# Token table of the expert layer by one-hot matrix products instead of indirect DMAs, with the mixer's steps in a new order

## What is computed

```python
# 1. linear attention, 16 heads of 32, in chunks of 128 tokens, with a decayed state
x = layernorm(x + rms_norm(lightning_attn(rotary(x @ Wq), rotary(x @ Wk), x @ Wv)) @ Wo)

# 2. a selective scan over the context (512 inner channels, 16 states), gated by silu(x)
u = silu(conv1d(in_proj_w @ ctx, conv_w) + conv_b)          # 4 taps, causal
dt_low, Bm, Cm = split(x_proj_w @ u, [16, 32])
dt = softplus(dt_proj_w @ dt_low + dt_proj_b)
for t in range(512):
    state = state * exp(dt[t] * A) + (dt[t] * u[t]) * Bm[t]
    y[t] = (state * Cm[t]).sum(states)
x = layernorm(x + ((y + D * u) * silu(x)))

# 3. experts: 64, each token goes to its best 8; an expert takes at most 256 tokens
probs = softmax(x @ router_weight.T)
topw, topi = top_k(probs, 8);  topw /= topw.sum()
pos = place of (token, choice) in its expert's list, in order of tokens
xe[topi, pos] = x                      # where pos < 256
ye = (silu(xe @ gate) * (xe @ up)) @ down
y = sum over the 8 choices of ye[topi, pos] * topw          # 0 where pos >= 256
x = layernorm(x + y)
```

## Time and profile before

| | us |
|---|---|
| median of 3 runs (1345.42 to 1348.79) | 1347.47 |
| the profiled execution, its own time | 1349.46 |
| its span in the profile | 1347.6 |

### The profile page before, as it was taken

The page is one execution under the profiler, slowest core; times in us unless marked ns, Lnnn a source line. Parts: engine busy times, 40 slices in busy tenths (PEclk is TensorE's granted clock), DMA queues, the critical chain, the costliest instruction groups (busy, mean ns, idle before and its releaser), DMA issues. The chain is left out here.

```text
span 1347.6 us, 19321 instructions
## 1 busy us (share of the span) xinstructions
PE 1138.9 (85%) x6389; PEld 757.4 (56%) x6389; DVE 1100.1 (82%) x1536; ACT 853.8 (63%) x1536; POOL 1003.9 (74%) x796
## 2 busy tenths in 40 slices
PE   7489997898979779967887718999999999999950
PEld 2234443354424434433443418999999999999940
DVE  2379988989968799878798566998888989898846
ACT  5474585734756444847345326888878888888843
POOL 0778768777899997999988744777777777777644
PEclk9698887997889789878978658999999999999985
DMA  6525425323242432163133306999999999999978
GB/s 244 140 72 191 110 65 145 99 70 83 49 111 61 124 84 51 46 154 106 38 83 102 98 13 208 302 315 305 308 304 306 305 313 301 313 301 311 285 138 326
DMA packets 97490, 235.26 MB, mean 175 GB/s; under 512 B 20704, under 2 KB 21216, under 8 KB 96752
## 3 DMA queue, kind: packets, MB, share of 16 engines
q1 hardware_dynamic: 65648, 162.66, 39.5%
q0 software_dynamic: 31744, 71.37, 22.3%
HBM read 147.48 MB, written 52.94 MB: 149 GB/s over the span
## 5 line engine op out<-in xcount | busy, mean ns | idle before, releaser
L1226 DVE TENSOR_TENSOR_SCAN hst<-hst,dbu 128x512 f32<-128x512 f32 x256 | 299.2, 1214 | 97.1 <-POOL dbu L1035 71.8
L1035 POOL TENSOR_TENSOR dbu<-rep,bc 128x1024 f32<-128x1024 f32 x128 | 301.8, 2360 | 64.1 <-PE y_ps L396 35.3
L1642 POOL DMA_INDIRECT sum_rows<-ye,tokens x128 | 205.5, 1606 | 98.4 <-ACT ye L1721 75.6
L396 PE MATMUL y_ps<-dbu,cs 128*32 128x512 f32 x512 | 167.8, 741 | 70.3 <-DVE dbu L1232 62.6
L799 ACT ACTIVATE hst<-rep,small_sb 128x512 f32<-128x512 f32 x256 | 165.9, 685 | 56.8 <-DVE dbu L1232 51.5
L1634 POOL DMA_INDIRECT xe<-x_rows,tokens x128 | 150.6, 1176 | 61.4 <-issue 37.8
L434 PE MATMUL ring<-first_raw,xT 128*128 128x512 f32 x384 | 176.7, 604 | 0.5 <-DVE x2T L1314 0.5
L1232 DVE TENSOR_TENSOR dbu<-hst,bc 128x1024 f32<-128x1024 f32 x128 | 156.7, 1224 | 4.4
L1684 PE MATMUL low<-xh,w1h 128*128 128x256 f32 x512 | 150.5, 294 | 0.0
L1684 PE MATMUL low<-xh,w1l 128*128 128x256 f32 x512 | 145.3, 284 | 0.0
L1684 PE MATMUL low<-xl,w1h 128*128 128x256 f32 x512 | 145.2, 284 | 0.0
(11 more groups left out here) (198 smaller groups left out, 2680.0 us busy)
## 6 DMA issues: line engine op xcount, KB each, us to landing
first_raw<-in_gate_up SPq DMA_DIRECT2D x64, 768.0 KB, 9.8
rep<-made SPq DMA_DIRECT2D x256, 128.0 KB
second_raw<-in_down SPq DMA_DIRECT2D x64, 256.0 KB, 5.1
bc<-bc_rows SPq DMA_DIRECT2D x64, 128.0 KB, 3.2
second_raw<-in_down SPq DMA_DIRECT2D x64, 128.0 KB, 7.2
rows<-sum_rows SPq DMA_DIRECT2D x16, 512.0 KB, 8.9
sum_rows<-x2T SPq DMA_DIRECT2D x1, 4608.0 KB, 17.2
xT<-in_x_turned SPq DMA_DIRECT2D x16, 256.0 KB, 3.0
```

The lines of the kernel that those rows point to most:

```text
L396: ins = pe.matmul(y_ps[rows, :], sel, dbu[:, n % WORK, g, :], start=(k == 0), stop=(k == QUADS - 1))
L1035: pool.tensor_tensor(dbu[:, n % WORK, :, :], rep[:, i % 2, :, 1, :], bc[:, k, 0, :].unsqueeze(1).broadcast_to([P, 2, T]), ALU.mult).then_i ...
L1226: dve.tensor_tensor_scan(h, h, dbu[:, n % WORK, i, :], 0.0, ALU.mult, ALU.add).then_inc(scanned, 1)
L1642: pool.indirect_dma_start(sum_dram[e % SUMS], bass.IndirectOffsetOnAxis(ap=tokens[:, e, j:j + 1], axis=0), ye[:, e % YE, j, :], None, comp ...
```

## The change

- **All sequences' tables on chip.** The DRAM tables, the indirect DMAs, `tell_slots` and `split_slots` go. `number_slots` (DVE) splits each slot number into a high half (expert and 128-block) and a low half (0 to 127), both as f16 in `place_of`. For each of the 16 chunks, one one-hot matrix of 128 places x 8 choices is made of each half, and eight f16 matmuls of 128x128 add up high x (low times token number).
- **For sequences 0 to 2** there are twelve such jobs, spread over the slots by `HOTS`. A job that is due in slot n: DVE makes the high half after its scan n (`number_tokens`, 128x1024 f16); POOL subtracts a count from the low places behind `inputs(n + 1)` (`part_lows`, 128x1024 f16); ACT makes |difference| and then relu(token - token x |difference|) behind `decays(n + 2)` (`peak_lows`); PE multiplies behind `sum_states(n + 2)` (`place_tokens`, one more use of the ring); DVE adds the 128x128 result to the table behind scan n + 3 (`add_slots`). Jobs of sequence r are due in (c 3, k 1), (c 3, k 4) of the sequence r+1 and in (c 0, k 1), (c 0, k 4) of r+2; for r = 2 in (c 2, k 1), (c 2, k 4), (c 3, k 0), (c 3, k 3) of sequence 3.
- **For the last sequence** DVE makes both halves (`place_last`, eight instructions), with a count that was laid out in full beforehand (`count8`), ACT multiplies by the token's number (four instructions of 128x1024), PE does 32 matmuls, DVE adds, fills in the spare numbers and writes `tokens` in three instructions of 128x128. `experts` no longer loads, joins or turns anything.
- **Order.** `project_context`, `first_tap` and `convolve` go from slots 2 to 5 of step 2 to its slots 0 to 3, `gate_u`, `project_u` and the taking of `xdbl` follow sooner; `soften`, `exponentials` and `logs` go one slot forward in step 3; the rounding part of `logs` becomes `rounded`, one slot behind; `soft_parts(b+1, 0)` and `soft_rest(b+1, 0)` go one slot forward on POOL, `steps_of_u(b+1, 0)` goes ahead of `rotate`; the second tile's `excess`, `steps`, `soft_rest` and `steps_of_u` go behind the border of the sequences; `gate_z(b, 2)` joins `gate_z(b, 3)` in the next step 0; `exponents` and `turn_rows` go forward a slot; `count_places` goes back one.

The core of the diff:

```diff
+HOT_AT = ((0, 3, 1), (0, 3, 4), (1, 0, 1), (1, 0, 4))
+HOT_LAST = ((0, 2, 1), (0, 2, 4), (0, 3, 0), (0, 3, 3))
...
+            def place_tokens(r, j):
+                pe.wait_ge(lows_numbered, NT * r + j + 1)
+                pe.wait_ge(hots_made, NT * r + j + 1)
+                ps = to_fill(pe, f"slots{r}_{j}")
+                for k in range(TOPK):
+                    ins = pe.matmul(ps[:, 0:P], hot[:, hot_place(j), 1, :, k], hot[:, hot_place(j), 0, :, k],
+                                    start=(k == 0), stop=(k == TOPK - 1))
+                ins.then_inc(fill_sem(f"slots{r}_{j}"), 1)
...
-            sp.wait_ge(slots_ready, 2)
-            sp.dma_start(last_dram.rearrange("(g p l) -> p g l", p=P, l=ROW), slots_of[:, :, :]).then_inc(slots_stored, 16)
-            sp.wait_ge(slots_stored, 16)
...
+            def peak_lows(r, j):
+                lows, at = hot[:, hot_place(j), 1, :, :], NT * r + j
+                act.wait_ge(lows_apart, at + 1)
+                act.activation(lows, lows, ACT.Abs).then_inc(lows_distant, 1)
+                act.wait_ge(lows_distant, at + 1)
+                act.activation(lows, lows, ACT.Relu, bias=cs[:, C_TOK + at:C_TOK + at + 1], scale=less[:, at:at + 1])\
+                    .then_inc(lows_numbered, 1)
...
-            def scatter(b, first, end):
-                if first == 0:
-                    pool.wait_ge(routed, b + 1)
-                for n in range(min(first, NT * TOPK), min(end, NT * TOPK)):
-                    pool.indirect_dma_start(table_dram, bass.IndirectOffsetOnAxis(ap=idx_s[:, n:n + 1], axis=0),
-                                            tok_i[:, NT * b + n // TOPK:NT * b + n // TOPK + 1], None).then_inc(scattered, 16)
+            def part_lows(r, j):
+                pool.wait_ge(placed, r + 1)
...
+                shape = [P, P, TOPK]
+                pool.tensor_tensor(hot[:, hot_place(j), 1, :, :], place_of[:, 1, j, :].unsqueeze(1).broadcast_to(shape),
+                                   count16[:, :].unsqueeze(2).broadcast_to(shape), ALU.subtract).then_inc(lows_apart, 1)
...
-                        if k == 4 and c == NT - 1 and not last:
-                            soft_parts(b + 1, 0)
+                        if k == 3 and c == NT - 1 and not last:
+                            soft_parts(b + 1, 0)
+                        if k == 4 and c == NT - 1 and not last:
+                            soft_rest(b + 1, 0)
...
+            def make_hots(r, j, hots, count, parts):
+                dve.wait_ge(placed, r + 1)
+                for h in parts:
+                    ins = dve.tensor_tensor(hots[:, h, :, :], place_of[:, h, j, :].unsqueeze(1).broadcast_to([P, P, TOPK]),
+                                            count, ALU.is_equal)
+                ins.then_inc(hots_made, 1)
...
+            def place_last(own):
+                own.settle()
+                for j in range(NT):
+                    make_hots(B - 1, j, hot_last[:, j], count8, (0, 1))
+                taken(dve, f"slots{B - 2}_{NT - 1}")
+                ps = full(dve, f"slots{B - 1}")
+                spares = key[:, 0:2, :].rearrange("p j e -> p (j e)").rearrange("p (e j) -> p e j", j=CJ)
+                own.step(dve.tensor_tensor(tokens_f, ps[:, 0:P].rearrange("p (e j) -> p e j", j=CJ), tokens_f, ALU.add))
...
-            pe.wait_ge(table_float, 1)
-            pe.transpose(turn_ps[0][:, 0:P], tab_f[:, :], ident).then_inc(table_turned, 1)
-            pe.wait_ge(tokens_ready, 1)
```

More of the change, by code:

```diff
@@ L89, with hots_due, hot_place @@
 NORM2_STEPS = NT
-ROUTE_STEPS = 25
-LAST_STEPS = 15
+ROUTE_STEPS = 27
+HOT_AT = ((0, 3, 1), (0, 3, 4), (1, 0, 1), (1, 0, 4))
+HOT_LAST = ((0, 2, 1), (0, 2, 4), (0, 3, 0), (0, 3, 3))
+HOTS = {SLOT_COUNT * (r + 1 + over) + UNIT * c + k: (r, j)
+        for r in range(B - 1) for j, (over, c, k) in enumerate(HOT_LAST if r == B - 2 else HOT_AT)}
+def hots_due(n, later=0):
+    return (HOTS[n - later],) if n - later in HOTS else ()
+def hot_place(j):
+    return 1 if j < 2 else 0
 def wait(eng, sem, value):
@@ L738, in _ @@
                             store_x2(b - 1)
-                        if c == 1 and k == 6 and not last:
+                        if c == 1 and k == 4 and not last:
                             load_context(b + 1)
@@ L744, in _ @@
                             clear_sums()
-                        if c == NT - 1 and k == 1 and not last:
+                        if c == NT - 1 and k == 0 and not last:
                             store_rows(b + 1)
@@ L802, in first_tap @@
             def first_tap(b, m):
-                if m == 0:
-                    wait(act, routed, b - 1)
+                if b >= 3 and m < 2:
+                    full(act, f"slots{b - 3}_{NT - 1}")
                 if m == 0 and b == 0:
@@ L818, in soften @@
             def soften(b, tiles):
+                if tiles == LATE and b >= 2:
+                    full(act, f"slots{b - 2}_1")
                 for m in tiles:
@@ L919, in _ @@
                     decays(n + 1)
+                    for r, j in hots_due(n + 1, 2):
+                        peak_lows(r, j)
+                    if front:
+                        first_tap(b + 1, 0)
                     if soft:
-                        act.wait_ge(bc_stored, 16 * (b + 1))
-                        take(f"xdbl{b + 1}", xdbl[:, :])
+                        soften(b + 1, EARLY)
+                    if c == 0 and b:
+                        excess(b, 1)
+                        steps(b, 1)
+                    if c == 1:
+                        excess(b, 2)
                     if back and c == 1:
@@ L951, in _ @@
                         take_rows(b - 1, 1)
-                    decays(n + 4)
+                    decays(n + 3)
+                    for r, j in hots_due(n + 3, 2):
+                        peak_lows(r, j)
                     if front:
-                        first_tap(b + 1, 1)
+                        first_tap(b + 1, 2)
                     if soft:
                         logs(b + 1, EARLY)
+                    if c == 1:
+                        steps(b, 2)
+                    take_mixed(t)
                     if back and c == 1:
                         take_rows(b - 1, 2)
+                    decays(n + 4)
+                    for r, j in hots_due(n + 4, 2):
+                        peak_lows(r, j)
+                    if front:
+                        first_tap(b + 1, 3)
+                    if soft:
+                        rounded(b + 1, EARLY)
+                    if c == 1:
+                        steps(b, 3)
+                    if back and c == 1:
                         take_rows(b - 1, 3)
+                        exponents(b - 1)
                     if more:
@@ L1158, in _ @@
                         n = SLOT_COUNT * b + UNIT * c + k
-                        if c == NT - 1 and k == 6 and not last:
-                            steps_of_u(b + 1, 0)
                         if n + 1 < SLOT_COUNT * B:
                             inputs(n + 1)
+                        for r, j in hots_due(n):
+                            part_lows(r, j)
                         if k == 0 and t:
@@ L1186, in _ @@
                         if k == 5 and c == NT - 1 and not last:
-                            soft_rest(b + 1, 0)
+                            steps_of_u(b + 1, 0)
+                        if k == 5 and t + 1 < NT * B:
+                            rotate(t + 1)
                         if k == 6 and c == NT - 1 and not last:
                             soft_parts(b + 1, 1)
-                        if k == 7 and c == NT - 1 and not last:
-                            soft_rest(b + 1, 1)
-                        if k == 5:
-                            mixed_root(t)
@@ L1194, in _ @@
-                        if k == 5 and t + 1 < NT * B:
-                            rotate(t + 1)
-                        if k in (6, 7) and c == 0:
-                            soft_parts(b, k - 4)
+                        if k == 0 and c == 0 and b:
+                            soft_rest(b, 1)
+                            steps_of_u(b, 1)
+                        if k == 7 and c == 0:
+                            soft_parts(b, 2)
+                        if k == 0 and c == 1:
+                            soft_parts(b, 3)
```

409 lines of the change are left out of this document (199 added, 210 removed).

## The result

The changed kernel is slower: 1363.3 us (median of four runs, 1359.45 to 1366.05) against 1346.7 (1345.42 to 1348.79) on the same chip, ratio 1.012, 95% interval 1.0091 to 1.0148. The forecast was 1325.5. The profiled execution took 1359.45 us, the lowest of its four, with a span of 1357.4 against 1347.6 before.

A forecast was written before the change was run, and what follows sets the result against it. DVE was taken to set the mixers' pace, with 96.7 us of stalls; -22.5 + 24 - 13.5 - 10 = -22 us from 1349.46 gave 1327.5, as a median 1325.5 us, range 1313 to 1334.

The forecast's parts named there:

- Part A: Mixers: removing the indirect DMAs gives back what made DVE late, -22.5 us, bounds -15 and -26.
- Part B: Mixers: the twelve new jobs cost DVE 17.5 us plus 6 of port waits, +24 us, bounds +17 and +41.
- R2: Rival, mixers: the job relay holds the steps up, 1.1 us more per job, 13 in all, 1338.5 us; chance 0.22.
- Part C: Mixers: the new order of the loops removes waits, -13.5 us in sum, bounds -24 and 0.
- C3: Step 2: the convolution in slots 0 to 3 is the same DVE work in another place, 0 us by itself.
- C2: Border between sequences: POOL's copies come out sooner and one DVE wait nearly goes, -4 us.
- C1: Step 1: `exponents` a slot sooner ends DVE's 2.50 us wait for it, -7.5 us.
- C4: Step 0 of sequence 0: two `excess` leave and the rounding goes a slot later, so DVE waits less, -2.5 us.
- Part D: End of the mixers, up to POOL's first gather: the table made on chip shortens it, -10 us, bounds -5.5 and -11.
- R1: Rival, mixers: all of POOL's lateness and half of ACT's go, -46 us, 1301.5 us; chance 0.12.
- R3: Rival, mixers: GpSimd's subtraction costs 4.7 us, twice the assumed, up to 28 us more, 1353.5 us; chance 0.08.
- R4: Rival: no change in sum, the port's worst (+17) and no fast form at the end (+4), 1346.5 us; chance 0.05.

The follow-up runs named there:

- e3: The changed kernel with the loops in the order of before and without the twelve jobs: 1321.1 us, ratio 0.9807 to the kernel before.
- e7: The changed kernel with only DVE's and GpSimd's instruction of each job, without ScalarE's passes, TensorE's matmuls and the adding: 1333.9 us, ratio 0.9883 to before.
- e4: The changed kernel with the twelve jobs' one-hots laid out slot index innermost, so TensorE's matmuls read neighbours: 1349.2 us, ratio 1.0012 to before.
- e5: e4 with the last of each sequence's four jobs in slot 6 of step 0 instead of slot 4: 1346.3 us, ratio 0.9979 to before.
- e2: The changed kernel, new order kept, without the twelve jobs: 1314.3 us, ratio 0.9756 to the kernel before.
- e9: e5 with ScalarE's taking of `xdbl` moved behind the decays at the end of step 2: 1341.2 us, ratio 0.9952 to before.
- e10: e5 with convolution, projections, first taps and gate back in their old slots of step 2, `xdbl` taken in slot 0 of step 3: 1346.8 us.
- e1: The changed kernel with its jobs and end, but every loop in the order of before: 1374.1 us, ratio 1.0197 to before.
- e13: e9 with each sequence's jobs at slot 1 of step 3, slots 0 and 4 of step 0, slot 1 of step 1: 1340.0 us, ratio 0.9952 to before.

## Why the prediction was wrong, point by point

**Part A held.** Step 1 of sequences 2 and 3 went from 54.8 to 47.4 us. Leaving out the first step, whose length varies, the mixers of e3 are 22.9 us shorter than before; the sum said 22.5 (its terms add up to 22.7). With the first step they are 18.8 us shorter.

**Part B is the step that failed: +24 against 50.3.** Its terms one by one: DVE's 17.5 + 6 came out as 26.1, GpSimd's subtraction as 2.30 (2.36 forecast), ScalarE's passes as 2.28 per job, all in their bounds. The term that was wrong is TensorE's: "eight f16 matmuls, about 1 us", taken over without the step of eight elements between their columns, and "about a slot to spare" for what stands behind. They took 2.06 us, and there was no slot to spare. The sum priced the relay at nothing beyond DVE's own work; e7 shows 1.2 us of new idle time without the relay, and the whole kernel 24.2. e4 gives 10.0 of them back (and 3.7 of DVE's busy time), e5 5.9 more. Outside the first step the jobs cost 48.3 us, 24 more than the sum: TensorE's operands are 14.4 of these (e4), the shared half of `hot` 4.3 (e5), and some 6 stay open. R2 named this ("the relay holds the steps up") with "a longer pass on ACT, or the port" as its cause, and put 1.1 us per job on it; it is 2.0 from the idle time alone, and the cause is TensorE's operands and the shared half of `hot`. The clock that falls behind TensorE's stalls adds to it by the rows, but no run takes it apart. What I wrote would make the forecast wrong, "if PE's ring stops it in step 0", comes nearest to what happened; DVE and GpSimd waited there for the buffer in `hot`.

**Part C: the sum was too good, its terms wrong in both directions.** C3, the convolution, was set at 0 and costs 13.4 us. C2, the border, was set at -4 and brings 12.1 in e2 against e3 (5.0 in steps 3, 7.1 in steps 0). The two look like one exchange, in which the border gets what step 2 loses; e9 and e10 speak for it, since steps 3 and 0 grow where step 2 falls. C1 said -7.5 and steps 1 fell by 2.3: the wait for the exponents is gone (8.0 us before, 0.5 now, over four times), but DVE's busy time there rose from 41.8 to 43.0 us. The new order puts two of DVE's instructions beside GpSimd's: `chose` takes 1.27 us in sequences 0 to 2 of e2 and 0.29 in e3, and the adding to `prev` 0.90 instead of 0.22; both end about 0.1 us behind a GpSimd instruction. C4, the first step, was set at -2.5 and gives 5.1 and 9.7 in the two pairs, and its own spread of 3 to 4 us doesn't allow to tell closer. In all -13.5 was forecast, and 7 (e3 and e2) to 11 (e1 and changed) were found. All of the first and more than half of the second are the first step; the other terms gave 0 to 4 us and not the 11 of the sum.

**Part D held**: 9.9 us shorter from the last product to the first gather (51.4 and 41.5), 10 forecast. The fast form was right, 0.61 us measured and 0.62 forecast; the eight matmuls behind ScalarE's last pass were 1.1 in the sum, and from that pass's end at 810.92 to the adding it is 4.3: at 1.9 us for eight, the same mistake as in Part B, TensorE falls behind the passes.

**Part E held**: the first product is at 53.33 us, 0.4 earlier (in other kernels with the new order at 53.5 to 56.4). The experts took 2.0 us less.

**The rivals.** R1's idea that lateness vanishes with GpSimd's load falls: GpSimd has 48 us less to do, and DVE's waits for it went from 71.8 to 61.8 us only; without the wait ahead of the first scan (31.3 and 31.4), from 40.5 to 30.4. R3's price isn't there, 2.30 us and not 4.7. R4 was called R2 with the port's worst, but its sum left R2's 13 us out. The cases with a slower kernel held 0.08 between them, all on GpSimd's subtraction; the true one sat on TensorE and what waits behind it, at 2 us per job instead of R2's 1.1.

The best kernels here that put all tokens into the table are e9 and e13, 0.9952 of the time before (0.9933 to 0.997 and 0.9935 to 0.9969): the same change with whole runs for TensorE, the taking of `xdbl` behind the decays and, in e9, the fourth job later; e13 places the jobs in slot 1 of step 3, slots 0 and 4 of step 0 and slot 1 of step 1.

## What to carry to other kernels

Price a relay by its slowest link and by who waits behind each link, not by the work that it adds to the engine that sets the pace; two jobs that share a buffer need the distance of the whole relay, with room. Look at the access pattern of every matmul operand before taking its duration from another row: a layout that is convenient for the engine that writes can treble the time of the one that reads. A wait on ScalarE or TensorE costs what is queued behind it, so put a copy whose data may be late behind the work that the next slot needs; but measure the whole, since of the 8.6 us that this took out of three steps only 3.5 reached the sum.

## What the runs showed of the hardware

f16 matmuls of 128x128 whose operands step by eight elements took 257 ns each in a row, with neighbours 77 ns. A DVE instruction with two SBUF inputs that took 0.68 us alone took 1.75 in the median and up to 2.85 beside GpSimd's 2.36 us instructions: 20 of the 24 ended 0.55 us behind the end of a GpSimd instruction, whatever they took. After 2.2 us without work TensorE's clock was 0.50 and eight matmuls of 128x512 took 6.17 us instead of 3.68.
